# A selective-scan layer and a mixture-of-experts layer on one core: where VectorE makes each quarter's B product, and which PSUM banks take the token rows' transposes

## The reference, cut to what matters

```python
# layer 1, a selective scan (d: 1024 channels, n: 16 states)
xn = rmsnorm(layernorm(x)); xs, res = split(xn @ W_in)
xs = silu(causal_conv4(xs)); dt_r, B, C = split(xs @ W_xp)
delta = softplus(dt_r @ W_dt + b_dt)
h[t] = h[t-1] * exp(delta[t] * A) + delta[t] * B[t] * xs[t]   # for each of d x n
y[t] = sum_n h[t] * C[t] + xs[t] * D
x = x + (y * silu(res)) @ W_out + layernorm(x)
# layer 2: 32 experts, top 4, and a shared expert, on the normed rows
flat = rmsnorm(layernorm(x)); scores = softmax(flat @ router_w.T)
x = x + layernorm(x) + sum_k w_k * expert_k(flat) + shared(flat)
```

## Time and profile before

| | us |
|---|---|
| median of 3 runs | 1603.29 (1600.17 to 1603.88) |
| the profiled execution, its own time | 1605.29 |
| its span | 1603.2 |
| TensorE busy | 1447.4 (90%) |
| VectorE busy | 1309.0 (82%) |
| GpSimd busy | 1077.9 (67%) |
| ScalarE busy | 741.7 (46%) |

### The profile page before, as it was taken

How to read it: one execution, slowest core, us unless ns; L and a number is a source line. 1 busy time by engine, 2 the same in 40 slices (tenths; PEclk the granted TensorE clock), 3 DMA queues, 4 the chain that set the end, 5 groups by cost and what they waited for, 6 DMA issues and landing times.

```text
span 1603.2 us, 14721 instructions
## 1 busy us (share of the span) xinstructions
PE 1447.4 (90%) x4412; PEld 722.7 (45%) x4413; DVE 1309.0 (82%) x1931; ACT 741.7 (46%) x1160; POOL 1077.9 (67%) x545
## 2 busy tenths in 40 slices
PE   7678998899999898998899787899999999999997
PEld 3233443334444333443333333444445666667775
DVE  4599999899999999899999999344565877778772
ACT  4566665767565766666666665331000112111111
POOL 0199899899888899899999999250002455555553
PEclk9889999999999999999999999999999999999999
DMA  4550112510112510101510002231402788988995
GB/s 132 217 182 9 37 39 92 205 34 28 40 32 73 229 35 28 41 24 58 192 35 28 10 20 98 74 112 33 183 27 86 202 232 224 262 228 250 257 254 70
DMA packets 63822, 176.85 MB, mean 110 GB/s; under 512 B 10304, under 2 KB 15168, under 8 KB 55040
## 3 DMA queue, kind: packets, MB, share of 16 engines
q1 hardware_dynamic: 48128, 138.59, 25.1%
q0 software_dynamic: 15616, 37.32, 11.2%
HBM read 142.98 MB, written 32.85 MB: 110 GB/s over the span
## 4 chain that ended last, share of the span: by engine, by line
PE 49%; POOL 24%; DVE 14%; issue 5%; ACT 4%; DMA 4%; SPq 0%; POOLq 0%; DVEq 0%; ACTq 0%
POOL h L1361 13%; PE bank L1913 11%; PE bank L1562 9%; DVE h L952 8%; PE bank L1523 7%; PE bank L1955 5%; PE bank L1459 4%; POOL h L1348 3%; PE bank L1530 3%; PE bank L1491 3%; POOL h L1366 3%; DVE h L942 3%; DMA out<-y,slot_token 3%; PE bank L1481 2%; DVE xs L921 2%
## 5 line engine op out<-in xcount | busy, mean ns | idle before, releaser
L1361 POOL TENSOR_TENSOR h<-h,c_rep 128x2048 f32<-128x2048 f32 x128 | 579.3, 4530 | 34.7 <-DVE h L952 29.7
L1562 PE MATMUL bank<-h,ident 128*128 128x512 f32 x916 | 450.9, 636 | 94.9 <-POOL h L1361 74.0
L723 ACT ACTIVATE bank<-delta,a_neg 128x512 f32<-128x512 f32 x512 | 335.9, 683 | 181.9 <-DVE h L952 181.2
L1562 PEld LDWEIGHTS bank<-h,ident 128*128 128x128 f32 x916 | 180.5, 202 | 338.2 <-issue 211.3
L952 DVE TENSOR_TENSOR_SCAN h<-bank,state,h 128x512 f32<-128x512 f32 x256 | 306.0, 1263 | 0.2 <-ACT bank L723 0.2
L952 DVE TENSOR_TENSOR_SCAN h<-bank,h 128x512 f32<-128x512 f32 x256 | 290.8, 1202 | 2.0 <-ACT bank L723 2.0
L173 DVE STREAM_TRANSPOSE xT<-xg 32x256 f32<-32x256 f32 (+1 forms) x592 | 247.1, 417 | 18.3 <-DMA xg<-flat,slot_token 10.6
L942 DVE TENSOR_TENSOR h<-bank,b_rep 128x2048 f32<-128x2048 f32 (+1 forms) x105 | 227.7, 2187 | 36.7 <-ACT bank L714 24.9
L1913 PE MATMUL bank<-xT,w_ring 128*128 128x256 f32 x1024 | 227.4, 380 | 0.0
L1913 PEld LDWEIGHTS bank<-xT,w_ring 128*128 128x128 f32 x1024 | 193.8, 190 | 41.2 <-issue 16.6
L1722 POOL DMA_INDIRECT out<-y,slot_token x64 | 101.5, 1586 | 104.0 <-DMA out<-y,slot_token 71.0
(11 more groups left out here) (236 smaller groups left out, 1459.2 us busy)
## 6 DMA issues: line engine op xcount, KB each, us to landing
w_ring<-in_w SPq DMA_DIRECT2D x32, 1024.0 KB
b_rep<-bcd SPq DMA_DIRECT2D x16, 1024.0 KB, 6.7
c_rep<-bcd SPq DMA_DIRECT2D x16, 1024.0 KB, 4.8
w_ring<-in_w SPq DMA_DIRECT2D x32, 512.0 KB
w_in<-in_w_in_x SPq DMA_DIRECT2D x32, 256.0 KB, 2.6
w_res<-in_w_in_res SPq DMA_DIRECT2D x32, 256.0 KB, 2.6
xa<-in_x SPq DMA_DIRECT2D x20, 256.0 KB, 3.0
xb<-in_x SPq DMA_DIRECT2D x16, 256.0 KB, 3.0
```

The costliest lines, as they stand in the source:

```text
L723: eng.activation(da[j][:], delta[:, g % 2], ACT.Exp, scale=a_neg[:, col:col + 1])\
L1361: ins = eng.tensor_tensor(h[:, q], h[:, q], c_rep[:, Q * q:Q * q + Q, :], ALU.mult)
L1562: ins = eng.matmul(y_ps[:], c.ident[:], h[:, q, j, :], start=False, stop=(q == NQ - 1 and j == Q - 1))
```

## The change

1. On VectorE, each quarter's B product is moved to directly ahead of that quarter's scans. Before, it stood one quarter earlier: spread 1, scans 0, spread 2, scans 1, gate, spread 3, scans 2, scans 3, spread 0 of the next group. Now: scans 0, spread 1, scans 1, spread 2, gate, scans 2, spread 3, scans 3, spread 0.
2. In the closing stage the transposes of tiles 0 to 3 take work 2 to 5 (the decay banks) and those of tiles 4, 6, ..., 14 take work 7 (the bank of the sums); the others keep work 0 and 1. The count that tells when those buffers were last used before (opened) is now taken ahead of the closing items.
3. The list of closing items is in a new order: the transposes come in pairs with an output product, a router product or the first gate product between, the first pair ahead of the first output product. VectorE's copies, and two of ScalarE's copies (last_out), follow in the same order. The shared expert's first product of gate and up on VectorE, mult(0), is now behind the last logits.

```diff
--- before.py
+++ after.py
@@ -353,9 +353,9 @@
             ft, lg, lt = (lambda t: ("ft", 0, t, 0)), (lambda n: ("lg", 0, n, 0)), (lambda n: ("lt", 0, n, 0))
             gate, up = (lambda i: ("gate", 0, i, 0)), (lambda i: ("up", 0, i, 0))
             dn, rt = (lambda i: ("dn", 0, i, 0)), (lambda i: ("rt", 0, i, 0))
-            items = [last(0, 1), last(1, 1), ft(0), last(2, 0), ft(1), last(2, 1), ft(2), ft(3), last(3, 0), ft(4), lg(0), ft(5),
-                     last(3, 1), lt(0), ft(6), ft(7), ft(8), lg(1), ft(9), gate(0), lt(1), ft(10), ft(11), lg(2), up(0), lt(2)]
-            items += [ft(12), ft(13), ft(14), ft(15), lg(3)]
+            items = [ft(0), ft(1), last(0, 1), last(1, 1), ft(2), ft(3), last(2, 0), lg(0), ft(4), ft(5), last(2, 1), lt(0), ft(6), ft(7),
+                     last(3, 0), lg(1), ft(8), ft(9), gate(0), last(3, 1), lt(1), ft(10), ft(11), up(0), lg(2)]
+            items += [ft(12), ft(13), lt(2), ft(14), ft(15), lg(3)]
             routing = {4: 1, 7: 3, 10: 6, 11: 7, 12: 8, 13: 9}
             for u in range(1, UNITS):
                 items += [gate(u)] + ([lt(3)] if u == 1 else []) + [up(u)]
@@ -365,10 +365,17 @@
             return items
 
         closing = closing_items()
-
-        where, uses, held, turn = {}, [0] * 8, None, 0
+        for t in range(TT):
+            if t < ST:
+                spread_out["ft", 0, t] = 2 + t
+            elif t % 2 == 0:
+                spread_out["ft", 0, t] = 7
+
+        where, uses, held, turn, opened = {}, [0] * 8, None, 0, None
         for it in opening + [it for g in range(LAST + 1) for gap in gap_items(g) for it in gap] + closing:
             key = it[:3]
+            if it == closing[0]:
+                opened = uses[2:8]
             if it[0] in UNBANKED:
                 continue
             if key in spread_out:
@@ -384,8 +391,6 @@
             uses[turn] += 1
             if it[0] in HALVED:
                 held = turn
-
-        opened = uses[2:8]
 
         def was_free(eng, b):
 
@@ -845,12 +850,12 @@
                 flat_root(0)
                 for t in range(4):
                     flat_row(t)
-                last_out(0)
-                last_out(1)
                 flat_var(1)
                 flat_root(1)
+                last_out(0)
                 for t in range(4, 8):
                     flat_row(t)
+                last_out(1)
                 flat_var(2)
                 flat_root(2)
                 residual(NSEG - 1, 2)
@@ -976,18 +981,18 @@
                 for g in range(LAST + 1):
                     s, d = divmod(g, DC)
                     front(g - 1, 1)
-                    spread(g, 1)
                     scans(g, 0)
                     if d == 6:
                         statistics(s + 2, (0, 1))
+                    spread(g, 1)
+                    scans(g, 1)
                     spread(g, 2)
-                    scans(g, 1)
                     gate(g - 1)
-                    spread(g, 3)
                     scans(g, 2)
                     front(g - 1, 3)
                     if d == 6:
                         statistics(s + 2, (2, 3))
+                    spread(g, 3)
                     scans(g, 3)
                     front(g, 0)
                     if g < LAST:
@@ -1245,28 +1250,30 @@
                     flat_aggregate(g)
                     if g == 0:
                         gate(LAST)
-                flat_stat(12)
                 flat_turned(0)
                 flat_turned(1)
+                flat_stat(12)
+                flat_turned(2)
+                flat_turned(3)
                 flat_stat(13)
-                for t in (2, 3):
-                    flat_turned(t)
+                logits_out(0)
+                flat_turned(4)
+                flat_turned(5)
                 flat_stat(14)
-                flat_turned(4)
-                logits_out(0)
-                flat_turned(5)
+                flat_turned(6)
+                flat_turned(7)
+                logits_out(1)
+                flat_turned(8)
+                flat_turned(9)
                 flat_stat(15)
                 flat_aggregate(NSEG - 1)
-                for t in range(6, 10):
-                    flat_turned(t)
-                logits_out(1)
                 flat_turned(10)
                 flat_turned(11)
                 logits_out(2)
-                mult(0)
                 for t in range(12, TT):
                     flat_turned(t)
                 logits_out(3)
+                mult(0)
                 route_scores()
                 for u in range(1, UNITS - 1):
                     if u % HC == 0:
```

## The result

The changed kernel took **1584.88 us** (median of four runs, 1580.36 to 1588.19), the kernel before 1601.73 beside it: 16.8 us less by the medians. The ratio over all runs is 0.990, 95% interval 0.9882 to 0.9918, so 16.0 us less by it (13 to 19). The prediction said 1583, 1576 to 1593, and 20.7 us less than the profiled execution. The time lies in the range, but 4 to 5 us of the gain are missing, and the runs of the changed kernel lie 8 us apart where the runs of before lay 4 apart. Where they went is what the experiments had to find.

A forecast was written before the change was run, and what follows sets the result against it. Bound: a chain of waits among TensorE, VectorE and GpSimd, with VectorE binding where convolutions mix in. 1605.3 - 14.0 (VectorE order) - 6.7 (behind the last gate) = 1584.6, less 2.0 for the median: 1583 us, range 1576 to 1593.

The forecast's parts named there:

- Own-engine wait: VectorE, scan part: a scan directly behind its own B product waits 0.13 us for it to be written.
- Slower: Rival, chance 0.04: waiting for a 128x2048 product costs more than for 511 columns; at 1.0 us each, 1615 us.
- the one at no cost: Rival, chance 0.08: VectorE's 22 waits on its own products cost nothing, giving 1580 us.
- Opening: Start of the scan part: scans(0, 0) begin earlier, but GpSimd's spread(0, 3) still needs late B rows; gain 1.6 us.
- The GpSimd starvations at groups 8, 10 and 16: GpSimd's idles of 1.81, 1.60 and 0.86 us vanish; gains 3.0 us entering s = 1, 0.9 entering s = 2.
- The rounds at the end: Last groups of the scan part: rounds don't run through VectorE, stay at 26.92 us and gain nothing.
- Part one in all: VectorE's new order in the scan part: terms sum to 14.0 us gained, 2.9 more with waits at 0.
- The rival that starved moments move: Rival, chance 0.15: scan part's starved moments move instead of going; half of part one lost, 1590 us.
- The later gate priced at nothing: Scan part: the gate comes 0.26 us later, priced at nothing, or 0.26 us a group if cover is gone.
- Part two: Behind the last gate: TensorE's idle falls from 8.07 to 1.9 us, plus 0.5 less slow starts; gain 6.7 us.
- The rival that the change does nothing behind the gate: Rival, chance 0.07: extra buffers don't matter behind the gate; 1 to 2 us gained in place of 6.7, 1588 us.
- The rival TensorE starts faster: Rival, chance 0.05: shorter idle ahead of TensorE's sums makes them faster, 1.5 us more in s = 3; 1581 us.

The follow-up runs named there:

- after_again: The changed kernel run and profiled a second time, no edit: 1586.42 us, ratio 0.9916 to the kernel before.
- order_only: The kernel before with only VectorE's order in the scan part changed, nothing behind the last gate: 1590.38 us, ratio 0.9933 to the kernel before.
- the pair with earlier rescalings: Changed kernel, and closing part alone on the kernel before, both with GpSimd's rescalings of rows 0 to 9 moved earlier: 1580.84 and 1592.43 us.
- after: First profile of the changed kernel, no further edit: profiled execution 1580.36 us, median of the kernel's four runs 1584.88 us.
- rescale_early: The changed kernel with GpSimd's rescalings of rows 0 to 9 moved ahead of its last segment's statistics: 1580.84 us, ratio 0.9878 to the kernel before.

## Why the prediction came out as it did

- *Own-engine wait*: 0.13 predicted, 0.12 measured, on products four times as long as the convolutions from which it was taken. Right; the rival *Slower* and the one at no cost both fall.
- *Opening*: 1.6 predicted; 0.9 to 1.6 in the profiles. The first C product came as said (9.3 us behind the first du, 13.3 before), and the load of B rows set the rest, as said.
- *The GpSimd starvations at groups 8, 10 and 16*: gone, as said. *The rounds at the end*: 26.9 us still (TensorE's sum of quarter 2 starts at 907.05 and at 933.95), right, but not each: the last round takes 28.3 in this profile, since that sum at 933.95 took 5.12 us in place of 3.70, at a granted clock of 0.57 between 933 and 937 us; in after_again it takes 26.9.
- *Part one in all*: 14.0 predicted, 13.0 by the means of the profiles, 10.7 (8.0 to 13.4) by the runs of order_only and 11.7 by the pair with earlier rescalings. The sum was about right and, by the runs, 2 to 3 us too high. Its terms were right in sum rather than each: by the du times of after the gain stands at 10.4 us at group 13, where my terms give 6.4 (1.6, 1.8 and 3.0), and between groups 22 and 24 it loses 3.3 of it (13.5 to 10.2), where GpSimd waits 1.49 and 2.97 us for TensorE's sums. About half of that is the clock again: the sum ahead of the second wait took 5.40 us, and in rescale_early the same wait is 1.25. The rival that starved moments move has that much truth in it.
- *The later gate priced at nothing*: TensorE's wait for it more than doubled, and taking that away brought no gain that the runs can show. Supported, not proven.
- *Part two*: 6.7 predicted, 7.6 in every profile with the whole of it, 7.8 by the runs once the collision is gone. Right, a little low: idle left 1.56 us for 1.9, and 1.1 us less of slow starts (busy 44.83 to 43.74) where I took 0.5. The rival that the change does nothing behind the gate falls.
- *The rival TensorE starts faster*: nothing speaks for it. The mean granted clock is 0.967 to 0.972 in the runs of after_again and 0.968 to 0.972 in those of before beside them.
- **The step that failed** is the sentence in part two that GpSimd's rescaling comes later and that its readers are the stores, "needed only at the gathers, 100 us on". I asked who reads what the moved work writes, not whose instructions it now runs beside. The casts stood 0.02 us behind the rescalings in the trace of before, and the move put them inside, at 7.0 to 7.6 us where the hard form comes. That is most of the missing part of the gain: with the overlap 16.0 and 13.4 us (0.990 and 0.9916), without it 19.5 (17.3 to 21.9). Both profiles of the changed kernel itself have the mild form; that its slower runs (to 1593.6 us) had the hard one is inferred, from the variants with the same closing part and from the four runs with the same order and without the overlap, none of which is above 1582. Against 20.7 predicted the last is within its interval.
- *The baseline*: I took 2.0 us off for the median. The three sessions of before give 1600.6, 1600.6 and 1601.3, so the profiled execution (1605.3) stood 4 to 5 us above it. This error and the missed collision have opposite signs, which is why 1583 looks better than its working: that it lies so near is partly luck.

## What to carry to other kernels

When a change delays a block of work, list what it will run beside, on the other engine of VectorE and GpSimd above all, and look at the gap that it had: two rows 0.02 us apart in a trace are a warning. Before a gain of 1% is read off two profiles, cut both at a few fixed events; here one column held still to 0.1 us, one had two levels 7 us apart, and one wandered by 8. And a wait is worth nothing until it is shown that something waits for that engine: 28 us of TensorE's wait for the gate went away, 23 came back as a wait for GpSimd, and no gain showed. Where the wait is on the path, it can cost more than its length: 4.8 us of TensorE standing cost 7.2, with the slow matmuls behind.

## What was not expected of the hardware

- A VectorE instruction of 0.22 or 0.69 us took 9.29 or 8.82 us, blocked through seven or eight GpSimd instructions in a row; in other profiles, with the same instructions in the same places to 0.03 us, it was let in after one (0.68 to 1.31 us). What chooses was not found.
- The same eight matmuls behind the same wait (3.28 and 3.29 us), in two kernels with the same order of the scan part, ran at the full clock in one profile and partly at half in the other, 3.70 against 5.40 us.
